# Narrow attention: two key tiles weighed together in every second slot, the value projection one slot later

## The reference

```python
Q, K, V = split_heads(query @ Wq.T), split_heads(keys @ Wk.T), split_heads(values @ Wv.T)
scores = einsum('bhqd,bhkd->bhqk', Q, K) * scale + bias
scores = where(mask == 0, -inf, scores)
m = max(scores, axis=-1)
e = exp(scores - m)
attn = e / (1.0 + sum(e, axis=-1))          # layer 3: a softmax, without the 1.0
out = einsum('bhqk,bhkd->bhqd', attn, V)    # "the weighing" of the values
x = x + tanh(g) * (out @ Wo.T)
```

## Time and profile before

| | |
|---|---|
| median of 3 runs | 1465.39 us (1463.68 to 1467.89) |
| the profiled execution, device time | 1463.88 us |
| its span, first to last instruction | 1462.1 us |
| TensorE busy | 1284.2 us, 88% of the span |
| VectorE busy | 996.0 us, 68% |
| ScalarE busy | 811.8 us, 56% |
| GpSimd busy | 687.8 us, 47% |
| mean granted TensorE clock | 0.921 of full speed |

### The profile page before, as it was taken

One profiled execution on the slowest core, in us unless ns is written; L12 is line 12 of the kernel. 1 busy time (PEld: TensorE's weight loads), 2 busy tenths in 40 slices (PEclk: granted clock), 3 DMA queues, 4 the chain that ended last, 5 costly groups with the idle time before them and its releaser, 6 DMA issues. The chain is left out here.

```text
span 1462.1 us, 32229 instructions
## 1 busy us (share of the span) xinstructions
PE 1284.2 (88%) x11864; PEld 764.0 (52%) x11872; DVE 996.0 (68%) x3093; ACT 811.8 (56%) x1191; POOL 687.8 (47%) x630
## 2 busy tenths in 40 slices
PE   6999968836999999999984499999799966999994
PEld 4444444632666666666663145555467752555542
DVE  4988846136667666766557588888365676888866
ACT  2777732333656565656544367777553312777773
POOL 4667613521667667766762445241150027545411
PEclk8999987975999999999996689999999995999997
DMA  4556553534544144323003855440130005534301
GB/s 156 189 221 228 205 200 107 168 101 146 222 152 167 38 159 159 116 86 146 2 1 61 178 125 137 119 122 15 50 59 1 1 8 110 101 78 85 62 7 30
DMA packets 91078, 157.73 MB, mean 108 GB/s; under 512 B 15529, under 2 KB 60740, under 8 KB 87343
## 3 DMA queue, kind: packets, MB, share of 16 engines
q1 hardware_dynamic: 86440, 126.39, 29.8%
q10 hardware_dynamic: 2688, 25.56, 4.5%
q0 software_dynamic: 1808, 3.83, 1.2%
HBM read 99.16 MB, written 50.62 MB: 102 GB/s over the span
## 5 line engine op out<-in xcount | busy, mean ns | idle before, releaser
L2106 DVE CUSTOM_DVE_ANT_0 a_junk<-a_psM,a_madd 128x512 bf16<-128x512 f32 x480 | 312.9, 686 | 64.5 <-issue 57.7
L2049 ACT ACTIVATE a_probs<-a_psE 128x1024 f32<-128x1024 f32 x256 | 262.0, 1024 | 102.2 <-PE a_psE L1907 98.4
L2493 DVE TENSOR_REDUCE a_mx<-a_psM 128x1 f32<-128x512 f32 x236 | 148.2, 669 | 124.4 <-PE a_psM L2317 124.4
L1872 PE MATMUL a_psM<-narrow_k_op,narrow_q_op 57*64 57x512 bf16 (+1 forms) x960 | 194.1, 410 | 13.9 <-DMA narrow_q_op<-a_y_parts 8.7
L2454 ACT ACTIVATE a_probs<-a_psE 128x1024 f32<-128x1024 f32 x128 | 130.8, 1024 | 85.9 <-PE a_psE L2339 82.6
L2287 POOL TENSOR_TENSOR a_half_sum<-a_probs 128x1024 f32<-128x1024 f32 x64 | 150.7, 2355 | 32.7 <-ACT a_probs L2454 32.7
L1919 PE MATMUL a_psO<-a_probs,narrow_values 128*32 128x256 f32 x2048 | 163.7, 393 | 1.2 <-ACT a_probs L2049 1.2
L1898 PE MATMUL a_psE<-narrow_q_op,narrow_k_op 60*64 60x256 bf16 (+1 forms) x2048 | 155.4, 281 | 10.1 <-DMA narrow_q_op<-a_max_parts 10.1
L1907 PE MATMUL a_psE<-a_maddT,res_identb 64*64 64x512 bf16 x512 | 149.2, 386 | 0.0
L1907 PE MATMUL a_psE<-a_maddT_cross,res_identb 64*64 64x512 bf16 x512 | 147.1, 386 | 0.0
L2335 PE MATMUL a_psE<-a_qT,a_kT 64*128 64x256 f32 x1024 | 134.0, 381 | 0.0
(11 more groups left out here) (395 smaller groups left out, 2658.7 us busy)
## 6 DMA issues: line engine op xcount, KB each, us to landing
wide_k<-a_k_stage SPq DMA_DIRECT2D x32, 512.0 KB, 2.6
a_k_part<-wide_k SPq DMA_DIRECT2D x64, 256.0 KB, 2.9
wide_v<-a_v_stage SPq DMA_DIRECT2D x24, 512.0 KB, 4.1
a_kT<-wide_k ACTq DMA_DIRECT2D x6, 2048.0 KB
a_values<-wide_v ACTq DMA_DIRECT2D x6, 2048.0 KB, 8.5
keys<-a_parts SPq DMA_DIRECT2D x96, 64.0 KB
narrow_k_op<-keys SPq DMA_DIRECT2D x30, 192.0 KB
narrow_q_op<-a_queries SPq DMA_DIRECT2D x28, 192.0 KB
```

Of the source, the lines that this page charges most:

```text
L1872: last = pe.matmul(max_bank(s, j, first)[c * n:(c + 1) * n, :], q_op[r][group, s // 2, s % 2 * P + c * n:s % 2 * P + (c + 1) * n], k_op[r] ...
L2049: act.activation(probs[:, head:head + 2, k:k + 2, :], psE[es % 2][:], ACT.Exp).then_inc(exped, 1)
L2106: dve.tensor_tensor_reduce(junk[j][:], max_bank(s, j, first), madd[r][:, t, :], 1.0, -3.0e38, ALU.add, ALU.max, mx[r][:, max_place(h, t):m ...
L2493: dve.tensor_reduce(mx[r][:, at:at + 1], max_bank(2 * p + t, j, first), AX.X, ALU.max).then_inc(max_read, 1)
```

## The change

`weigh` is no longer called once in every slot, but twice in every slot with an odd `es` (an even `s`), for key tiles `es % 4 - 1` and `es % 4`; slots with an even `es` weigh nothing. The value projection moves from slot 11 to slot 12, on TensorE and, with it, its copy on ScalarE. Nothing is added or left out.

```diff
-        MAX_SLOTS, READ_SLOT, OUT_SLOT, INVERT_SLOT, BACK_SLOT, PROJECT_SLOT, V_SLOT = (8, 0), 0, 2, 3, 5, 7, 11
+        MAX_SLOTS, READ_SLOT, OUT_SLOT, INVERT_SLOT, BACK_SLOT, PROJECT_SLOT, V_SLOT = (8, 0), 0, 2, 3, 5, 7, 12
...
-                        quad, t = es // QUAD - 1, es % QUAD
-                        if quad >= 0 and take_exp:
-                            weigh(w, at, quad, t, first)
-                        if quad < 0 and (inner or w >= 1):
-                            weigh(w - 1, (at - 1) % RING, QUADS - 1, t, False)
+                        quad = es // QUAD - 1
+                        for t in range(es % QUAD - 1, es % QUAD + 1) if es % 2 else ():
+                            if quad >= 0 and take_exp:
+                                weigh(w, at, quad, t, first)
+                            if quad < 0 and (inner or w >= 1):
+                                weigh(w - 1, (at - 1) % RING, QUADS - 1, t, False)
```

## The result

| | before | after |
|---|---|---|
| median | 1464.54 us (4 runs, 1462.42 to 1467.89) | 1487.74 us (4 runs, 1487.32 to 1490.86) |
| the profiled execution | 1463.88 us | 1487.57 us |

The change makes the kernel slower: ratio 1.0173, with a 95% interval of 1.0150 to 1.0196. The medians differ by 23.2 us (their quotient is 1.0158, within the interval), the profiled executions by 1487.57 - 1463.88 = 23.69 us; the forecast sum was +25.4.

The account below looks back on a forecast made before the run. TensorE was taken to set the pace, with VectorE's 1.20 us bank round hidden behind it until slots lose their weighing. Terms 23.4 + 4 - 2 = +25.4 on 1463.88 gave 1489 us, range 1472 to 1500.

Parts of the forecast that it names:

- What bounds the kernel: Steady slots: TensorE sets the pace at 1.35 us, hiding VectorE's 1.20 us round of one PSUM bank.
- The odd and the even slot: Plain slots: without weighing 1.20 us, with two key tiles 1.95; a pair 3.15 against 2.73.
- The whole step: Steps 2 to 7 of two layers: 27.32 us each against 25.37, +23.4 us in all.
- Moving the value projection: Slot 11 to 12: costs 0.55 us a step, 14 times, 7.7 us, already counted in the sum.
- Step 1: First step with weighing, lacking `turn_out`, `turn_back` and `project`: +2 us a layer, +4 in all.
- step 8: Step without maxima: TensorE gains 0.14 us a slot, ScalarE's exponentials leave 0.04; -1 us a layer, -2 in all.
- my two terms: Step 1, per layer: four plain pairs lose 1.7 us, the value projection's pairs (slots 10 to 13) lose 0.8.
- My upper bound of +16: Even slots: the second key tile costs at most 0.57 us, +0.14 for each of 128 - 16 pairs.
- TensorE's busy share: Steady stretch of a narrow layer: falls from 99% to about 80%.
- rival 1: All paired slots: TensorE alone sets the time, a pair takes 2.46 us against 2.73, kernel 1436 us; chance 0.11.
- 2, the second key tile in 0.21: Even slots: second key tile streams in 0.21 us, step 25.56, kernel 1466 us, no change; chance 0.06.
- 3, the clock falls: TensorE's idle gaps lower its clock to 0.50 in a tenth of 14 steps: +30 us more, 1520; chance 0.04.

Follow-up runs that it names:

- experiment 4: The changed kernel with VectorE's maximum over the last 128 of 512 columns and queries scaled by a further 0.05: 1437.33 us, ratio 0.9811.
- experiment 5: The kernel before and the changed kernel, each with maxima over the last 256 of 512 columns and the 0.05 scaling: 1445.59 us and 1440.58 us.
- experiment 3: The kernel before with VectorE's maximum over the last 128 of 512 columns and queries scaled by a further 0.05: 1449.89 us, ratio 0.9898.
- experiment 2: The changed kernel with the value projection back in slot 11 instead of 12: 1476.87 us, ratio 1.0082.
- experiment 6: The kernel before with key tiles weighed in pairs only in step 8, where no maxima are taken: 1453.89 us, ratio 0.9977.
- experiment 7: The kernel before with pairs only in slots 7 and 8, 11 and 12, and step 8 behind its first slot: 1451.74 us, ratio 0.9953.

## Why the prediction was right, step by step

**What bounds the kernel.** Right. TensorE sets the pace, and VectorE, tied to it by one bank for each head, takes over as soon as a slot has no weighing. Experiments 4 and 5 show it as a cause: with a shorter read the pairs went from +1.94 us a step to -0.07 and -0.86, and the whole kernel from +23.2 to -5.0 and -12.6. Besides the read only the scale of the values differed; no run changed it alone, but it is the same in each pair of runs, and the plain slot (1.35) and the two weighed tiles (1.00) take as long with it as without. One thing was put too strongly: that the read is hidden before holds for the plain slots, not for the whole step, which lost 0.55 us with a short read (experiment 3).

**The odd and the even slot.** Right to the hundredth: 1.20 forecast, 1.20 and 1.21 read; 1.95 forecast, 1.95 and 1.96 read; the second maximum held to 0.62 as forecast, and a second key tile at 0.43.

**The whole step.** Right: 27.32 and 27.32, though there is luck in the last digits, as errors cancel. Slot 0 took 2.03 and not 2.12, slot 15 took 1.30 and not 1.20, slots 7 and 8 took 1.42 and 1.95 and not 1.45 and 1.97. Slot 15 is about 0.09 longer than the other odd slots with the short reads too (0.89 and 1.03, experiments 4 and 5), so it isn't the read's length; the cause stays open. The term +23.4 measured +23.3.

**Moving the value projection.** Forecast 0.55 a step, 7.7 in all; taken back, it gave 0.61 a step (experiment 2), 7.65 us by the profiled executions and 10.9 by the medians. I had put the heavy slot behind the projection at 1.80 and it was 1.77, and the one with it at 1.89, where it was 1.87.

**Step 1 and step 8.** Forecast +4 and -2, so +2 in all; outside of the six steps of each layer the profiled execution grew by 23.69 - 23.33 = 0.4 us in all. Step 8 gained 1.5 a layer (experiment 6), -3.0 and not -2. This is the term that was mis-sized; it makes 1.0 of the 1.7 us between +25.4 and +23.7. The error is in the reading of the earlier trace rows: 3.31 / 3 = 1.10 divides by three what spans two intervals and one record, and (3.31 - 1.02) / 2 = 1.15, with 1.02 for one exponential, is only TensorE's own slot of 1.14, for which ScalarE waited. With pairs the last four went at 0.98 (experiment 6).

What is left, 0.4 + 3.0 = 3.4 against the +4 of step 1, is no clean measure of it, and that it comes near is in part luck. 1.2 us of it lie ahead of layer 2, where nothing was changed (its first maximum starts at 812.29 and not at 811.07), and from there the first scores of layer 2 came 2.6 us earlier than before. In slots 4 to 15 of step 1, away from that wait, the change cost 2.3 us a layer, where my two terms make 1.7 + 0.8 = 2.5.

**The range and the median.** My upper bound of +16 reaches 1505, and I let the range end at 1500 without a reason. The median that I thought might come out at 1491 was 1487.74.

**TensorE's busy share.** This reading failed: I expected about 80%, and the stretch shows 92%. There are two faults in it. I had taken the share of a plain pair for that of a step: a step of 27.32 holds 25.37 - 1.88 = 23.49 us of TensorE's own work by rival 1's count, 86% at most, since the 25.37 have waits in them too. And a record is longer than the time after which the next may start. Before, a maximum of 0.40 had its weighing start 0.33 behind it; in front of a wait that modelled end runs into the pause and counts as busy. The forecast of the time did not use the share.

**The rivals.** 1, TensorE alone sets the time: out at a read of 0.69 us, and it is what happens when the read is short. The Trainium skill, TensorEngine Tiling (Array Packing), Tiling Modes, says that a change of the tiling mode drains the array. The trace agrees in that a change has a price, 0.14 us; the drain itself is not seen in it. It became time saved only in the pair of slots 11 and 12 of experiment 2 and in experiments 4 to 7, where VectorE's loop was short, absent or covered. 2, the second key tile in 0.21: out, it took 0.43. 3, the clock falls: out, it was 1.00 in the stretch and 0.918 over the execution (0.921 before).

## What to carry to other kernels

Before you count a saving on the busiest engine, ask what its next instruction needs, and how long that takes through the other engine and back. Work in a slot that is shorter than this round costs nothing; take it out, and the slot stays as long as the round, while the slot that the work moves to gets longer. So cluster work of one array shape where the emptied slot holds something else of that length (slots 7 and 11), or where there is no round (step 8), and leave it spread elsewhere.

To find such a round in a trace, go by the starts of the instructions on both engines; busy shares don't show it. And a sum slot by slot, each from a row, came out within 0.1 us a slot here, where TensorE's busy share of 99% spoke for rival 1, a gain.

## What the runs showed of the hardware that I had not expected

**A busy share hides short waits.** The stretch shows 8% idle, and by the count above at least 14% of a step is idle. Pauses of a few tenths of a us, one in every slot or two, are partly covered by the modelled ends of the records before them.

**The read's cost by width.** `tensor_tensor_reduce` from PSUM took 0.69 us for 512 columns, 0.42 for 256 and 0.29 for 128: about 0.15 fixed and 0.105 for each 100 columns. The first halving saved 0.27 and the second 0.13.

**The next bound.** With a short read and pairs, TensorE stood still for 2.0 us once in layer 2, where it waits for the masks, and behind it the granted clock was 0.50 for some 3 us. In after, with waits of 0.36 us in every second slot, it stayed at 1.00. Whether the masks, prepared earlier, would give back the 4 us that layer 2 lost against layer 3 was not tried.
